# Second GCN layer's weight product in a fused GAT, GCN and LSTM kernel: the weight as the stationary side

## What is computed

```
h = jnp.maximum(_layernorm(x, axis=-1), 0.0)
x = x + _L0_gnn_ref(h, adj, L0_gnn_W, L0_gnn_a)          # graph attention
h = jnp.maximum(_layernorm(x, axis=-1), 0.0)
x = x + _L1_gnn_ref(h, adj, Wg0, bg0, Wg1, bg1, Wih, Whh, bih, bhh)
```

```
h = relu(adj @ (x @ Wg0 + bg0))
h = relu(adj @ (h @ Wg1 + bg1))
for p in 1, 2, 3, 4:
    last = lstm_last(Wih[p-1], Whh[p-1], bih[p-1], bhh[p-1], windows of p nodes of h)
    h[:, last node of each window] = last
```

## Time and profile before

| | |
|---|---|
| median of 3 runs | 462.01 us (460.8 to 462.74) |
| the profiled execution: its time / its span | 463.6 us / 461.8 us |
| TensorE matmuls busy | 437.6 us, 95% |
| VectorE busy | 379.1 us, 82% |
| ScalarE busy | 324.5 us, 70% |
| GpSimd busy | 76.8 us, 17% |
| mean granted TensorE clock | 0.979 |

### The profile page before, as it was taken

The page is one execution under the profiler, slowest core; times in us unless marked ns, Lnnn a source line. Parts: engine busy times, 40 slices in busy tenths (PEclk is TensorE's granted clock), DMA queues, the critical chain, the costliest instruction groups (busy, mean ns, idle before and its releaser), DMA issues.

```text
span 461.8 us, 8052 instructions
## 1 busy us (share of the span) xinstructions
PE 437.6 (95%) x2568; PEld 383.4 (83%) x2568; DVE 379.1 (82%) x973; ACT 324.5 (70%) x635; POOL 76.8 (17%) x182
## 2 busy tenths in 40 slices
PE   6579999979998999999989999999999999999995
PEld 5358888879997999999968888899999988887874
DVE  3799999986778887788776888888888788888895
ACT  3479999966787678788666687667667675565452
POOL 5758840330319200000000000000000000000000
PEclk9689999989999999999999999999999999999998
DMA  8900000000000000000000000000000000002116
GB/s 244 334 40 1 2 2 1 0 1 0 1 1 2 0 0 0 0 0 1 0 0 2 0 2 0 0 1 2 0 1 0 2 1 1 0 23 70 45 48 182
DMA packets 14075, 11.68 MB, mean 25 GB/s; under 512 B 982, under 2 KB 12252, under 8 KB 13788
## 3 DMA queue, kind: packets, MB, share of 16 engines
q1 hardware_dynamic: 11404, 9.97, 7.1%
q10 hardware_dynamic: 2640, 1.33, 1.1%
HBM read 7.10 MB, written 4.19 MB: 24 GB/s over the span
## 4 chain that ended last, share of the span: by engine, by line
PE 71%; DVE 17%; ACT 3%; DMA 3%; issue 3%; DVEq 1%; SPq 1%; ACTq 0%
PE ps L985 47%; PE ps L1107 12%; PE ps L1111 6%; DVE score L716 4%; DVE score L682 4%; DMA xs<-in_x 3%; DVE xs L730 2%; PE ps L965 2%; DVE stats L672 2%; ACT work L609 1%; ACT v_norm L504 1%; PE ps L948 1%; PE ps L1055 1%; PE ps L1029 1%; PE ps L1025 1%
## 5 line engine op out<-in xcount | busy, mean ns | idle before, releaser
L609 ACT ACTIVATE work<-ps,bl 128x512 f32<-128x512 f32 (+2 forms) x204 | 111.0, 628 | 30.8 <-PE ps L1111 23.4
L985 PE MATMUL ps<-h_hi,wl_hi 128*128 128x512 f32 (+3 forms) x252 | 94.7, 376 | 4.0 <-DVE h_lo L776 3.2
L985 PE MATMUL ps<-h_hi,wl_lo 128*128 128x512 f32 (+3 forms) x252 | 94.0, 373 | 0.0
L985 PE MATMUL ps<-h_lo,wl_hi 128*128 128x512 f32 (+3 forms) x252 | 94.0, 373 | 0.0
L599 ACT ACTIVATE work<-work 128x512 f32<-128x512 f32 (+2 forms) x56 | 31.5, 570 | 44.5 <-DVE work L860 33.7
L985 PEld LDWEIGHTS ps<-h_hi,wl_hi 128*128 128x128 f32 x252 | 47.6, 189 | 11.6 <-issue 3.1
L985 PEld LDWEIGHTS ps<-h_lo,wl_hi 128*128 128x128 f32 x252 | 47.8, 190 | 7.6
L504 ACT ACTIVATE v_norm<-xs,shift,scale 128x128 f32 (+1 forms) x128 | 52.6, 487 | 1.5 <-POOL shift L406 1.5
L985 PEld LDWEIGHTS ps<-h_hi,wl_lo 128*128 128x128 f32 x252 | 47.7, 189 | 6.5
L1107 PE MATMUL ps<-s_hi,wl_hi 128*128 128x512 f32 (+2 forms) x144 | 51.9, 362 | 0.0
L1107 PE MATMUL ps<-s_hi,wl_lo 128*128 128x512 f32 (+2 forms) x144 | 51.4, 359 | 0.0
(11 more groups left out here) (136 smaller groups left out, 975.3 us busy)
## 6 DMA issues: line engine op xcount, KB each, us to landing
result<-xs SPq DMA_DIRECT2D x12, 256.0 KB, 2.3
work<-in_w_ih_t SPq DMA_DIRECT2D x1, 1024.0 KB, 9.8
work<-in_w_hh_t SPq DMA_DIRECT2D x1, 1024.0 KB, 8.7
xs<-in_x SPq DMA_DIRECT2D x2, 256.0 KB, 3.6
xs<-in_x SPq DMA_DIRECT2D x1, 512.0 KB, 7.8
result<-xs SPq DMA_DIRECT2D x4, 128.0 KB, 2.4
result<-xs ACTq DMA_DIRECT2D x4, 128.0 KB, 2.8
adj_raw<-in_adj ACTq DMA_DIRECT2D x1, 256.0 KB, 6.7
```

Of the source, the lines that this page charges most:

```text
L609: nc.scalar.activation(lw[:, par, g, 0:cols], ps[:, 4 * par + g, 0:cols], ACT.Tanh if g == G else ACT.Sigmoid, bias=bl[:, (p - 1) * GATES ...
L985: ins = nc.tensor.matmul(dst, a, b, start=start and n_ == 0, stop=stop and n_ == 2)
```

## The change

In stage 3 the second weight becomes the stationary side, as in stage 2: three matmuls of 512 columns give the product with features on partitions, in bank 2. ScalarE adds the bias as a per-partition operand and writes the sum to a new SBUF tile `y1`; TensorE turns `y1` over in four transposes of 128x128 into PSUM bank 5 (`TURNED`, free in phase B, since only three of the four gates are used there). The high and low part of stage 3 are then read from bank 5. The bias matmul, its prepared operand and the DMAs for it go; one DMA brings the bias as a column. The orders of the three engines within a tick are rearranged.

```diff
@@ gpsimd
-            for k in range(4):
-                done(nc.gpsimd.tensor_copy(b1_parts[64:P, k], b_zeros[64:P]))
-                done(nc.gpsimd.tensor_copy(b1_parts[0:32, k], b_full[0:32, 1]))
-                done(nc.gpsimd.tensor_tensor(b1_parts[32:64, k], b_raw[32:64, 1], b_full[32:64, 1], ALU.subtract))
@@ scalar, phase_b
-                for s in (4, 3, 2, 1):
+                def part_hi(s):
...
+                    if s == 3:
+                        act.wait_ge(b_T, t - 2)
+                    else:
+                        act.wait_ge(b_mm[s], t - s + 1)
...
+                    nc.scalar.activation(dst, ps[:, TURNED if s == 3 else s - 1, :],
+                                         ACT.Copy if s in (1, 3) else ACT.Relu).then_inc(b_hi[s], 1)
+                part_hi(4)
+                if live(3):
+                    act.wait_ge(b_mm[3], t - 2)
+                    after(act, b_T, t - 3, 0)
+                    nc.scalar.activation(y1[:, :], ps[:, 2, :], ACT.Identity, bias=b1_col[:, 0:1]).then_inc(b_y, 1)
+                part_hi(2)
                 if live(0):
...
                     normalise(1, t, range(4), b_v)
+                part_hi(1)
+                part_hi(3)
@@ vector, phase_b
-                for s in (4, 3, 2, 1):
+                def part_lo(s):
...
+                part_lo(4)
+                part_lo(2)
                 if live(0):
...
                     nc.vector.tensor_tensor(s_lo[:, 0, :], v, s_hi[:, 0, :].bitcast(fp32),
                                             ALU.subtract).then_inc(b_lo[0], 1)
+                part_lo(1)
+                part_lo(3)
@@ tensor, phase_b
-                    after(pe, b_lo[s], t - s, 0)
+                    after(pe, b_y if s == 3 else b_lo[s], t - s, 0)
...
                     elif s == 3:
-                        nc.tensor.matmul(ps[:, s - 1, :], ones[:, :], b1_parts[:, :, :].rearrange("p k f -> p (k f)"),
-                                         start=True, stop=False)
-                        for k in range(4):
-                            c = slice(k * P, (k + 1) * P)
-                            ins = product(ps[:, s - 1, c], (hi[:, c], lo[:, c]), (wg_hi[:, 1, :], wg_lo[:, 1, :]),
-                                          False, k == 3)
+                        ins = product(ps[:, s - 1, :], (wg_hi[:, 1, :], wg_lo[:, 1, :]), (hi, lo), True, True)
...
+                if live(3):
...
+                    pe.wait_ge(b_y, t - 2)
+                    after(pe, b_lo[3], t - 3, 0)
+                    for k in range(4):
+                        ins = nc.tensor.transpose(ps[:, TURNED, k * P:(k + 1) * P], y1[:, k * P:(k + 1) * P], ident[:, :])
+                    ins.then_inc(b_T, 1)
```

More of the change, by code:

```diff
@@ L50, in preln_gat_gcn_lstm_kernel @@
     SKIPS = 4
-    GCN_LOADS = 10
+    GCN_LOADS = 8
     GATES = 4
@@ L94, in preln_gat_gcn_lstm_kernel @@
         wg_lo = sb("wg_lo", [P, 2, D], fp32r)
-        b_raw = sb("b_raw", [P, 2, D])
-        b_full = sb("b_full", [P, 2, D])
-        b_zeros = sb("b_zeros", [P, D])
+        b_raw = sb("b_raw", [P, D])
+        b_full = sb("b_full", [P, D])
+        b1_col = sb("b1_col", [P, 1])
+        y1 = sb("y1", [P, 512])
         b0_parts = sb("b0_parts", [P, D], fp32r)
-        b1_parts = sb("b1_parts", [P, 4, D], fp32r)
         rs_full = sb("rs_full", [P, N])
@@ L200, in preln_gat_gcn_lstm_kernel @@
         b_mm = [None] + [sem(f"b_mm{s}") for s in range(1, 5)]
+        b_y = sem("b_y")
+        b_T = sem("b_T")
         b_hi = [sem(f"b_hi{s}") for s in range(5)]
@@ L224, in preln_gat_gcn_lstm_kernel @@
         BESIDE = 4
+        TURNED = 4 + F
         def ticks(eng, depth, unroll, body, first=0, beside=None, lag=0):
@@ L353, in _ @@
             sp.wait_ge(b_zero, 1)
-            for l, b in enumerate((b_gcn0, b_gcn1)):
-                for r in (0, 32, 64):
-                    sp.dma_start(b_raw[r:r + 1, l, :], b.rearrange("(o f) -> o f", o=1)).then_inc(gcn_w_in, 16)
+            for r in (0, 32, 64):
+                sp.dma_start(b_raw[r:r + 1, :], b_gcn0.rearrange("(o f) -> o f", o=1)).then_inc(gcn_w_in, 16)
+            sp.dma_start(b1_col[:, :], b_gcn1.rearrange("(f o) -> f o", o=1)).then_inc(gcn_w_in, 16)
             def store(q, lo, hi):
@@ L382, in _ @@
                                     pattern=[[-1, P]], channel_multiplier=1).then_inc(ident_ok, 1)
-            done(nc.gpsimd.memset(b_raw[:, :, :], 0.0))
-            done(nc.gpsimd.memset(b_zeros[:, :], 0.0))
+            done(nc.gpsimd.memset(b_raw[:, :], 0.0))
             nc.gpsimd.nop().then_inc(b_zero, 1)
@@ L432, in _ @@
             nc.gpsimd.tensor_tensor(bl[:, :], bl_raw[:, 0], bl_raw[:, 1], ALU.add)
[L433 to L437, removed]
-            for k in range(4):
-                done(nc.gpsimd.tensor_copy(b1_parts[64:P, k], b_zeros[64:P]))
-                done(nc.gpsimd.tensor_copy(b1_parts[0:32, k], b_full[0:32, 1]))
-                done(nc.gpsimd.tensor_tensor(b1_parts[32:64, k], b_raw[32:64, 1], b_full[32:64, 1], ALU.subtract))
+            done(nc.gpsimd.tensor_copy(b_full[:, :].bitcast(fp32r), b_raw[:, :]))
+            done(nc.gpsimd.tensor_copy(b0_parts[0:32], b_full[0:32]))
+            done(nc.gpsimd.tensor_tensor(b0_parts[32:64], b_raw[32:64], b_full[32:64], ALU.subtract))
+            done(nc.gpsimd.tensor_copy(b0_parts[64:P], b_full[64:P]))
             nc.gpsimd.nop().then_inc(b_ok, 1)
@@ L571, in phase_b @@
                                              bias=bl[:, g:g + 1]).then_inc(one_act, 1)
-                for s in (4, 3, 2, 1):
+                def part_hi(s):
                     if not live(s):
-                        continue
-                    act.wait_ge(b_mm[s], t - s + 1)
+                        return
                     if s == 4:
@@ L580, in phase_b @@
                         dst = s_hi[:, s, :]
-                        after(act, b_mm[s + 1], t - s, 0)
-                    nc.scalar.activation(dst, ps[:, s - 1, :], ACT.Copy if s in (1, 3) else ACT.Relu).then_inc(b_hi[s], 1)
+                    if s == 3:
+                        act.wait_ge(b_T, t - 2)
+                    else:
+                        act.wait_ge(b_mm[s], t - s + 1)
+                    if s < 4:
+                        after(act, b_mm[s + 1], t - s, 0)
+                    nc.scalar.activation(dst, ps[:, TURNED if s == 3 else s - 1, :],
[6 more added lines that the diff above has]
+                part_hi(2)
                 if live(0):
@@ L773, in phase_b @@
                     if s in (1, 3):
-                        ins = nc.vector.tensor_tensor(dst, ps[:, s - 1, :], hi.bitcast(fp32), ALU.subtract)
+                        ins = nc.vector.tensor_tensor(dst, ps[:, TURNED if s == 3 else 0, :], hi.bitcast(fp32), ALU.subtract)
                     else:
@@ L1042, in phase_b @@
                     ins.then_inc(b_mm[s], 1)
+                if live(3):
+                    if isinstance(t, int) and t == 3:
+                        pe.wait_ge(a_pT, PAIRS)
+                    pe.wait_ge(b_y, t - 2)
[3 more added lines that the diff above has]
+                    ins.then_inc(b_T, 1)
             ticks(pe, 4, 4, phase_a, beside=phase_b)
```

## The result

The changed kernel takes 467.5 us in the median of four runs (467.09 to 468.26), the kernel before 462.17 beside it (460.8 to 462.74). The ratio is 1.0125, with a 95% interval of 1.0109 to 1.0141: slower, by 5.3 us. The profiled execution took 468.26 us, its span is 466.5, 4.7 more than before.

The account below looks back on a forecast made before the run. TensorE's matmuls, busy for 95% of the span, were taken to bound the kernel. 2.6 + 5.9 + 1.4 - 2.5 - 0.3 = +7.1 on the 462.0 median gave 469.1, raised to 469.3 for the entry's waits; range 464 to 475.5.

Parts of the forecast that it names:

- Entry: Tick 3, the first with stage 3: the following stage 4 starts at 120.5 instead of 117.85, costing 2.6 us.
- Steady ticks: From stage 4 of tick 4 to that of tick 16: twelve ticks, each 0.49 us longer, 5.9 us.
- Slow clock at the entry: TensorE idles some 3 us at entry, and a stretch at half clock follows: 1.4 us added.
- Weight split: GpSimd's LSTM weight split slows VectorE in two ticks; 1.1 us remains of 3.6 lost before, net -2.5.
- Tail: Ticks 16 to 18, bounded by TensorE, save 0.42 us each; tick 18's transposes add 0.9: net -0.3.
- End of phase B: The sum of all five terms, from entry to tail: phase B ends 7.1 us later.
- Rounds: The LSTM rounds after phase B: called untouched by the change, costed at nothing.
- The loop: Phase B: stage 2's high part, normalisation, stage 0, stage 3's low part, TensorE's stages 4, 3, 2: 7.95 us a tick.
- TensorE's own work: In a phase B tick: 7.46 less 2.50, plus 1.63 for products and 0.45 for transposes, 7.04 us.
- Transposes: Four added on TensorE per phase B tick: bounded by 0.40 and 0.55 us, taken as 0.45.
- The clock in the loop: Rival: TensorE's idle time in phase B's ticks lowers the clock; in all twelve, some 30 us more, chance 0.05.
- Faster: Rival: the way back in phase B's ticks is under 7.04, so TensorE's work ends last: 456.2 us, chance 0.07.

Follow-up runs that it names:

- three other traces of the early split: The kernel before with h_hi and h_lo both, h_lo alone, or h_hi alone moved to a multiple of 64 bytes: 458.92, 461.09 and 460.83 us.
- the traces with 1.82 and 1.87: The kernel before with h_lo alone, then h_hi alone, moved to a multiple of 64 bytes: 461.09 and 460.83 us.
- losing 0.61: The changed kernel with stage 3's parts ahead of stage 1's, both still behind the normalisation and stage 0: 460.25 us.
- losing all of it: The changed kernel with the parts of stages 1 and 3 put back ahead of the normalisation and stage 0: 455.96 us.

## Why the prediction was right, and which step was not

The forecast was 469.3 us in a range of 464 to 475.5, the measurement 467.5. The steps of the sum, by the profile:

| Step | forecast | measured |
|---|---|---|
| Entry | 2.6 | 120.31 - 117.85 = 2.46 |
| Steady ticks, 12 x (tick - 7.466) | 5.9 | 12 x 0.474 = 5.7 |
| Slow clock at the entry | 1.4 | 9.48 - 7.96 = 1.5 |
| Weight split | -2.5 | 1.0 left of 3.6: -2.6 |
| Tail | -0.3 | -0.4 |
| End of phase B | +7.1 | 239.65 - 232.75 = +6.9 |
| Rounds | 0 ("untouched") | 226.85 - 229.05 = -2.2 |

The five steps add up to 6.7; the 0.2 that are missing lie in the ticks behind the entry, 8.0 in place of 7.94. The 1.0 of the weight split is the sum of what its two ticks take above the steady ones (8.40 and 8.50, less twice 7.94). The tail is the difference of the lateness of stage 4 in tick 16, 7.3, to the 6.9 at the end.

The weight split came out at its forecast because both were taken against one execution of the kernel before. That one was 1.6 us above the median and had the half clock behind the split, which three other traces of the early split don't have; against their 2.6 the term is 1.0 - 2.6 = -1.6. By the medians the steps and the rounds then come to +5.7, beside the measured 5.3. That the forecast fell only 1.8 us too high is in part luck: the step that failed is 2.2 by itself, and the split's 0.9 err the other way.

**The loop** was right in place and length: 7.95 forecast, 7.93 to 7.95 measured. The cast of stage 0 came 2.17 behind the high part of stage 2, as forecast, and the low part of stage 3 ended at 4.52, not 4.54. Two small misses cancel: stage 4 started 0.06 behind VectorE, the lower of the two bounds, where 0.15 was taken, and from there to the next high part of stage 2 took 3.37 in place of 3.26, since the first matmul after the wait occupies 0.22 and not 0.12. That the order makes the loop is shown by taking it to the products of before (8.9 a tick) and away from those of after (7.01 to 7.06).

**TensorE's own work** was reckoned at 7.04 a tick; where it waits for nothing it is 7.01 to 7.06. Its idle time ahead of stage 4 was to be 0.9. The profile prints 0.66 to 0.67, counted from the modelled end of the last gate; from what that matmul occupies it is 0.82 (169.78 to 170.60).

**Transposes.** Four held TensorE 0.36 to 0.44, of the 0.40 to 0.55 forecast. "TensorE: Matmul & The Clock Gate", Part 4, of the Trainium skill, with about 275 ns each, is right about the time of one (0.60 from the first's start to the last's end, with 0.10 to 0.12 from start to start) and not about what four cost in a row.

**The rivals.** The clock in the loop: 1.00 over 44 us with a wait in each tick, so that the oscillation which the Trainium skill describes in the same page ("A second HAM failure mode: psum-queue depth-cycling") did not appear at these waits. In phase B it stood at half after the entry only, where filling the wait with matmuls kept it up. The forecast read the clock's fall from one idle time of 1.80; that this length is followed by half clock doesn't hold, as the traces with 1.82 and 1.87 show. Faster: the loop would have to lose 0.91 us, and losing 0.61 gave 7.34 ticks and 460.25 us, losing all of it 455.96. The forecast for that case was 456.2, and that they agree is luck in part, since the 455.96 hold the 2.2 us of the rounds, which the forecast had not.

It hid a part of the loss: at the placement of before the change costs 7.5 us, where 7.1 to 7.3 were worked out; measured as it stands, it costs 5.3. I had looked at what the removed tiles cost to fill, not at what their absence does to the addresses behind them.

## What to carry to other kernels

In a pipeline whose engines each run a fixed order, take a part that the next tick needs first, and follow it from its wait through everything queued ahead of it back to itself: if that loop is longer than the busiest engine's work, a saving on that engine buys nothing, and here the place of one instruction in the order was worth 7 us. When a change adds or drops a tile, compare the addresses of all tiles behind it, and time the change at equal placement, else a gain of placement is booked to the change. Work that slows another engine can't be hidden by moving it unless the place it goes to has slack on the slowed engine.

## What was unexpected of the hardware

- The pace of 512-column fp32r matmuls depends on where the moved tiles begin in SBUF: in the rounds 0.2267 us each at a multiple of 64 bytes, 0.2333 at 32 bytes behind one, and in phase B 0.229 and 0.233. It is worth 2.8 us in the kernel before, and most of it is lost when only one of the two tiles is moved. At 336 columns it is the other way round where it shows, 1.99 and 1.95 for twelve.
- A wait of 0.67 us (0.82 by occupancy) in every tick of 7.94 left the granted clock at 1.00; one of 2.8 us at the entry was followed by windows at 0.66 and 0.50. Single idle times of 1.80 to 1.87 were followed by 0.50 in one trace and by 1.00 in three.
- The first matmul after such a wait occupies 0.22 us in place of 0.12.
